# Six weight loads issued ahead of a barrier, and weight splitting and ranks reordered, in a sparse-attention and mixture-of-experts kernel

## What is computed

```python
h = _layernorm(x, axis=-1) * (1 + cb) + sb
x = x + gb * _L0_ffn_ref(h, router_w, router_b, w1, b1, w2, b2)

# in _L0_ffn_ref: 8 experts, 2 of them for each row
logits = xf @ router_w + router_b
topk_w, topk_i = jax.lax.top_k(jax.nn.softmax(logits, axis=-1), 2)
topk_w = topk_w / jnp.sum(topk_w, axis=-1, keepdims=True)
gates = zeros.at[rows, topk_i].set(topk_w)
h = jax.nn.relu(jnp.einsum('th,ehf->tef', xf, w1) + b1)     # 256 -> 1024
y = jnp.einsum('tef,efh->teh', h, w2) + b2                  # 1024 -> 256
out = jnp.einsum('te,teh->th', gates, y)
```

## Time and profile before

| | us |
|---|---|
| median of three runs | 1073.55 (1071.24 to 1073.58) |
| the profiled execution | 1073.43 |
| its span | 1071.6 |

### The profile page before, as it was taken

One profiled execution on the slowest core, in us unless ns is written; L12 is line 12 of the kernel. 1 busy time (PEld: TensorE's weight loads), 2 busy tenths in 40 slices (PEclk: granted clock), 3 DMA queues, 4 the chain that ended last, 5 costly groups with the idle time before them and its releaser, 6 DMA issues. The chain is left out here.

```text
span 1071.6 us, 26148 instructions
## 1 busy us (share of the span) xinstructions
PE 943.1 (88%) x7509; PEld 603.9 (56%) x7510; DVE 823.8 (77%) x2003; ACT 656.1 (61%) x1463; POOL 572.1 (53%) x582
## 2 busy tenths in 40 slices
PE   5998752699999999997688777999999999999995
PEld 3664442123333333332577336777788888888884
DVE  3677778789999999995667663777787777777773
ACT  3896776378988888886466583445444444444441
POOL 1347761737777777753766002444545445454533
PEclk9999995579999999998799697999999999999998
DMA  7126630521111111401587708988723323232322
GB/s 255 60 99 185 186 100 6 162 73 22 36 22 37 22 37 22 137 6 38 156 229 215 250 2 230 230 214 229 170 50 46 53 39 59 39 52 46 47 43 30
DMA packets 124954, 105.46 MB, mean 98 GB/s; under 512 B 17424, under 2 KB 118480, under 8 KB 124880
## 3 DMA queue, kind: packets, MB, share of 16 engines
q1 hardware_dynamic: 103024, 82.82, 25.9%
q0 software_dynamic: 20480, 20.67, 12.3%
q10 hardware_dynamic: 1376, 1.05, 0.3%
HBM read 50.13 MB, written 31.30 MB: 76 GB/s over the span
## 5 line engine op out<-in xcount | busy, mean ns | idle before, releaser
L1075 DVE TENSOR_REDUCE attend_mxh<-attend_p_a 128x1 f32<-128x512 f32 x416 | 257.1, 676 | 9.8 <-PE attend_p_a L1298 9.1
L2101 ACT ACTIVATE expert_hr<-expert_p,b1t 128x256 f32<-128x256 f32 (+1 forms) x376 | 134.1, 422 | 195.2 <-PE expert_p L2039 170.9
L1203 ACT ACTIVATE w<-attend_p_b 128x409 f32<-128x409 f32 x512 | 227.5, 515 | 37.4 <-PE attend_p_b L1312 35.4
L1994 POOL DMA_INDIRECT out_x<-expert_ys,expert_drop x72 | 125.1, 1738 | 190.5 <-DVE expert_ys L2136 136.6
L2061 PE MATMUL expert_p<-w,expert_hhi 128*128 x800 | 136.8, 273 | 0.7 <-DVE expert_ys L2136 0.3
L2039 PE MATMUL expert_p<-expert_xhi,w 128*128 128x256 f16 x800 | 136.4, 273 | 0.0
L1312 PE MATMUL attend_p_b<-attend_qb,w 64*128 64x409 f16 x512 | 130.8, 345 | 1.5 <-ACT w L1203 1.0
L1298 PE MATMUL attend_p_a<-w,attend_qa 64*128 64x512 f16 x384 | 123.5, 406 | 2.1 <-DVE attend_mxh L1075 1.3
L1984 POOL DMA_INDIRECT expert_xs<-h_d,expert_take x72 | 73.0, 1014 | 85.8 <-DVE expert_take L2140 64.8
L1338 PE MATMUL attend_p_o<-w,attend_vh 128*32 128x409 f32 x1024 | 116.4, 527 | 1.7 <-issue 0.7
L2061 PE MATMUL expert_p<-w,expert_hlo 128*128 x400 | 109.0, 273 | 0.0
(11 more groups left out here) (386 smaller groups left out, 1842.9 us busy)
## 6 DMA issues: line engine op xcount, KB each, us to landing
expert_wu<-w SPq DMA_DIRECT2D x88, 256.0 KB, 3.9
w<-in_L_ffn_w SPq DMA_DIRECT2D x30, 512.0 KB, 7.0
w<-in_L_attn_x SPq DMA_DIRECT2D x8, 512.0 KB, 10.9
q_d<-q SPq DMA_DIRECT2D x32, 128.0 KB, 1.7
k_d<-w SPq DMA_DIRECT2D x32, 128.0 KB
w<-k_d SPq DMA_DIRECT2D x32, 128.0 KB
attn_d<-zero SPq DMA_DIRECT2D x8, 512.0 KB, 5.8
route_ain<-attn_d SPq DMA_DIRECT2D x32, 128.0 KB, 3.6
```

Of the source, the lines that this page charges most:

```text
L1075: dve.tensor_reduce(mxh[q % 2][:, h, c, k:k + 1], p_a[chunk_use(q, a, h) % CB][:, :], AX, ALU.max).then_inc(a_done, 1)
L1203: act.activation(prob[:, 2 * (j % (TPB // 2)) + h, :], p_b[tile_use(p, j, h) % TB][:, 0:TOP], ACT.Exp, scale=SCALE / UNIT ** 2).then_inc(p ...
L1994: pool.indirect_dma_start(out=out, out_offset=bass.IndirectOffsetOnAxis(ap=drop[u][:, s:s + 1], axis=0), in_=ys[u][:, s, :], in_offset=Non ...
L2101: last = act.activation(hr[g % 2][:, f, rows], p_1[g][:, f, rows], ACT.Relu, bias=cst["b1t"][:, bass.ds(e[s] * FB + 2 * g + f, 1)], scale= ...
```

## The change

`w_here`, the semaphores on which the 12 weight loads land, and `raw_at` move from the slots block to `route_block` itself, as a set of their own that `places` hands out and clears. The first six loads are issued by SP in the routing block, behind its last save of h2 and ahead of its waits for the saves; the other six stay in the slots block. On ACT, Exp moves from behind piece 2 to behind high(1), and pieces up to high(7) and low(6) are done ahead of the tables; high(8) and low(7) stand between the tables where high(7) and low(6) stood. On PE, `LEFT_AT` becomes `(0, 0, 7, 7, 8, 9, 9)`: no piece ahead of the ranks and the far transpose, seven ahead of the spare product, none at group 0, one at group 1, one at group 2, none at group 3, three behind.

```diff
+        LOADS = [e * PIECES + c for e in range(E // 2, E) for c in range(PIECES if e < E - 2 else 2)]
+        AHEAD, SOON = 2, 6
+        _, _, kept_sem = places(nc, own, "weights")
+        w_here = [kept_sem(f"w_here{i}") for i in range(len(LOADS))]
+
+        def raw_at(n):
+
+            e, c = divmod(LOADS[n + AHEAD], PIECES)
+            if c < 2:
+                return cst["w1"][:, e, c, :, :].rearrange("p a f -> p (a f)").bitcast(F32)
+            return cst["w2"][:, e, (c - 2) * FB // 2:(c - 1) * FB // 2, :, :].rearrange("p b a n -> p (b a n)").bitcast(F32)
...
                 pipeline(sp, [load, None, None, None, save, None, None, save_h])
+                for n in range(SOON):
+                    sp.dma_start(raw_tile(raw_at(n), LOADS[n]), raw_of(io, LOADS[n])).then_inc(w_here[n], 16)
                 for c in range(4):
                     sp.wait_ge(h2_saved[c], 16 * NT // 4)
                     sp.wait_ge(x2_saved[c], 16 * NT // 4)
...
-            LEFT_AT = (1, 1, 6, 7, 7, 8, 8)
+            LEFT_AT = (0, 0, 7, 7, 8, 9, 9)
...
-                    for n in range(len(LOADS)):
+                    for n in range(SOON, len(LOADS)):
                         load(n)
...
-                    weights(0, 3)
+                    weights(0, 1)
+                    high(1)
                     act.wait_ge(dl_done, 1)
                     act.activation(ex[:, :], dl[:, :], ACT.Exp).then_inc(ex_done, 1)
-                    weights(3, 7)
+                    low(0)
+                    weights(2, 8)
                     act.wait_ge(slots_done, 1)
                     for g in range(GROUPS):
...
                         if g == 0:
-                            high(7)
+                            high(8)
                         if g == 1:
-                            low(6)
-                    for n in range(8, len(LOADS) + 1):
+                            low(7)
+                    for n in range(9, len(LOADS) + 1):
                         if n < len(LOADS):
                             high(n)
                         low(n - 1)
```

More of the change, by code:

```diff
@@ L1666, in route_block @@
             rank_ps, dl_done, ex_done = sem("rank_ps"), sem("dl_done"), sem("ex_done")
-            LOADS = [e * PIECES + c for e in range(E // 2, E) for c in range(PIECES if e < E - 2 else 2)]
             HALVES, WCOLS = 2, WCH // 2
-            LEFT_AT = (1, 1, 6, 7, 7, 8, 8)
-            AHEAD = 2
+            LEFT_AT = (0, 0, 7, 7, 8, 9, 9)
             wlast = [sb(f"wlast{i}", [P, WCH], F32) for i in range(AHEAD)]
+            raw_of_load = [raw_at(n) for n in range(len(LOADS) - AHEAD)] + [w[:, :] for w in wlast]
             p_w = [ps(f"p_w{i}", [P, 512], F32) for i in range(4)]
[L1674 to L1683, removed]
+            w_high, w_left, w_low = sem("w_high"), sem("w_left"), sem("w_low")
             def part_half(i, part, q):
@@ L1700, in load @@
                     def load(n):
-                        sp.dma_start(raw_tile(raw_at(n), LOADS[n]), raw_of(io, LOADS[n])).then_inc(w_here[n], 16)
-                    for n in range(len(LOADS)):
+                        sp.dma_start(raw_tile(raw_of_load[n], LOADS[n]), raw_of(io, LOADS[n])).then_inc(w_here[n], 16)
+                    for n in range(SOON, len(LOADS)):
                         load(n)
@@ L1714, in high @@
                         wait(act, w_left, HALVES * (n - AHEAD + 1))
-                        act.activation(weight_part(cst, LOADS[n], 0), raw_tile(raw_at(n), LOADS[n]), ACT.Copy, scale=WSCALE).then_inc(w_high, 1)
+                        act.activation(weight_part(cst, LOADS[n], 0), raw_tile(raw_of_load[n], LOADS[n]), ACT.Copy, scale=WSCALE).then_inc(w_high, 1)
                     def low(n):
@@ L1757, in left @@
                                 into = bank_half(HALVES * n + q, LOADS[n])
-                                raw = raw_at(n)[:, q * WCOLS:(q + 1) * WCOLS]
+                                raw = raw_of_load[n][:, q * WCOLS:(q + 1) * WCOLS]
                                 pe.matmul(into, minus[:, :], raw if LOADS[n] % PIECES < 2 else raw.rearrange("p (b n) -> p b n", n=D), start=True, stop=False)
```

## The result

The changed kernel takes 1078.77 us (median of 7, 1077.27 to 1081.19), the kernel before 1073.46 (median of 7 with the three from above, 1070.1 to 1075.47). The ratio is 1.0065, 95% interval 1.0052 to 1.0078: slower by 0.5 to 0.8%. The forecast was 1079.7.

A forecast was written before the change was run, and what follows sets the result against it. The prediction took the weight pieces on ACT and PE to set the slots block's end. +5.7 us at that end and +0.6 for the further clear made +6.3 on 1073.4: 1079.7 us, range 1073 to 1083.5.

The forecast's parts named there:

- What bounds the block: Slots block: the weight pieces on ACT and PE, not the routing, set the end, 4.1 us behind DVE.
- SP's six loads: Six loads issued ahead of SP's waits for the saves open the barrier later: +0.9 us, between 0.5 and 1.3.
- Ranks first, worth 0: Rank matmuls ahead of piece 0 put DVE's chain 3.45 us ahead, less 0.9; worth 0 on the path.
- A: Start of ACT's lane table 0: 621.7 instead of 618.6, +3.1 us, between 620.6 and 622.6.
- Behind A: Tables and tail: new wait at low(7), half clock in pieces 7 and 9, one piece fewer (-2.15); with A, +5.7 us.
- The further clear: The 12 semaphores' own set needs another clear with a barrier: +0.6 us, between 0.4 and 0.9.
- The table load: Ahead of Exp on ACT: load takes 1.28 us, without the skill page's 1.38 us drain; with it, forecast 1.4 us less.
- The gaps between bursts: PE between pieces 8 and 9: the skill's advice against idle gaps speaks against the change; clock down again, 1.75 us.
- Rival 1: Clock holds: pieces 7 and 9 on PE run at full clock, total 1075.1 us; chance 0.22.
- Rival 2: DVE's lead passes through: the block's end hangs on the routing chain, -4.1 us, total 1069.4; chance 0.09.
- Rival 3: SP hangs at one of the six issues, barrier opens 2.6 us later still, total 1082.3 us; chance 0.08.
- Rival 4: Nothing moves: waits at the block's ends swallow the change, total 1073.5 us; chance 0.05.

The follow-up runs named there:

- the version with two loads: Kernel before plus two early loads, semaphores from the slots block's set, ACT doing high(0), high(1), low(0), then Exp: ratio 0.9976 to before, run again 0.9975.
- one clear: Changed kernel with the 12 semaphores taken from the slots block's own set, so no further clear and barrier: ratio 1.0054 to the kernel before.

## Why the prediction was right, point by point

- **What bounds the block** held: the weight pieces end it. ACT's last copy ends 4.6 us behind DVE's drop table (648.90 against 644.34), and ACT began lane table 0 at least 1.1 us behind DVE's last slots in every run, so in none did DVE's lead decide when the tables begin.
- **SP's six loads**: forecast +0.9, measured +1.58. The mechanism was right, and the term too small. Six issues took 3.48 us, 0.58 each, where I took 0.46 from the loads in the slots block. The first two behind the saves take 0.46 each here too (0.92 in the version with two loads); it is the later ones that take longer, and why is open. The 1.3 that I gave as the upper bound was too low.
- **Ranks first, worth 0**: right. The matmuls ran at 603.29 and DVE's wait for them is gone, and lane table 0 did not come with it.
- **A**: forecast 22.94 + 2.2 behind DVE's start, measured 25.05. Its closeness is in part luck: in six more executions with seven pieces ahead it was 23.6 to 25.2, and in the five of them with ranks first 24.7 at most. The spread is the clock's first rise: from the first piece to A it was 18.26 us where the clock rose 5.1 us behind that piece (the changed kernel) and 16.80 where it rose 2.1 us behind (one clear). The parts of the term: the piece more cost 2.06 in its own run, and ranks first 0.3 behind DVE's start, with an early rise. Against them stands the stall that Exp caused ahead of piece 3 in the kernel before,

```profile
611.37 1.13 PE L1759 MATMUL slots_p_w<-w,minus 128*128 128x512 f32 x2 [1.03 <-ACT w L1715]
```

  of which there is none in the changed kernel, as forecast. So the move of Exp gave back about 1 us; it was not run alone.
- **Behind A**: table 3, piece 9 and the end were forecast 12.4, 16.2 and 25.3 behind, and came at 12.34, 16.56 and 26.07. The wait at low(7) was there, with piece 7 at half clock for 3.9 us (626.65 to 630.58) as forecast. How long the half clock lasted there was the mis-sized part: piece 9 starts 4.22 us behind table 3 instead of the forecast 3.8, and the pieces from it on lost 2.2 us, where I let them lose the 1.75 of piece 7, since the clock came back only at 643.8. The five executions with the wait at low(7) and no small matmuls end 25.8 to 26.1 behind A, though table 3 starts 12.3 behind it in three of them and 13.3 in two: the first and the second dip share the loss differently.
- **The further clear**: forecast 0.6, measured 0.87, inside its bounds of 0.4 and 0.9. The row that I took begins at the release of the barrier before and covers one clear; in the changed kernel the two clears begin 0.9 us apart (POOL's drains at L80, 649.1 and 650.0).
- **The sum** was +6.3; the block of the profiled execution grew by 7.9, the span by 7.4, the medians by 5.3. By the block, then, the terms were 1.6 us too small in all (0.7 SP, 0.8 behind A, 0.3 the clear, -0.1 A). That the total came within 1 us of the median all the same is luck in part: the profiled execution was 2.1 us above its median and had the latest first rise of the clock of all with ranks first, and no trace shows where a median execution is shorter. On another chip the same kernel was 9.2 us over before. In the first trace of the changed kernel the experts gave back 1.05 us: 429.4 us from their first copy to the span's end before, 428.3 after; their clock rose 4.6 us after their first matmul instead of 6.0.
- **The table load.** In the version with two loads it stands between a copy that ends at 602.03 and Exp, as in the earlier trace rows:

```profile
602.05 1.28 ACT L1739 ACT_TABLE_LOAD   x1
...
603.34 0.23 ACT L1739 ACTIVATE slots_ex<-slots_dl 128x32 f32<-128x32 f32 x1
```

  Exp starts 0.01 us behind the load. The drain of 1.38 us that the Trainium skill (ScalarE: Activation LUTs, What ACT_TABLE_LOAD costs) adds is on neither side of it; the measurement decides.
- **The gaps between bursts.** Filling them gave 4.3 us back. The advice of the Trainium skill (TensorE: Matmul & The Clock Gate, Why this matters for your kernels) to leave no long idle gaps between bursts of matmuls agrees with that.

Rival 1 (the clock holds) did not come by itself; made to hold, it gave the 21.79 that is near the 21.8 of its sum. Rival 2 (DVE's lead) is refuted. Rival 3, SP hanging at one issue, did not occur: 3.48 us for six. Rival 4, nothing moves, is out by the interval.

## What to carry to other kernels

Ask of every piece of work that is moved ahead who stands behind it in program order: here one more piece ahead of four tables and the wait between them that came with it cost 5 us, and a lead of 2 to 4 us on DVE was worth nothing, since another engine was late at that point already. Issues put in front of a barrier are free only as far as the wait behind them is long: two DMA issues fitted, six did not. And an early load is worth something only if an engine takes it at once. TensorE's idle gaps carry a price that shows only in the work behind them, so put the next piece there, or, as here, even products that nobody reads, and look at the granted clock of the stretch.

## What the runs showed of the hardware that I had not expected

Small matmuls whose result nobody reads made a stretch of the changed kernel faster: 24 of them (48 rows of about 0.27 us, which overlap) took 4.3 us off it, for the granted clock stayed at 1.00.

The rise of the clock came 2.1 to 5.6 us behind the start of the block's first piece in the thirteen profiled executions: 5.1 in the changed one, 4.1 in its second execution, 2.1 in the one with one clear (with ranks first, their products had begun 1.3 us ahead of the piece), and 5.4 in the kernel before. Each microsecond of it costs half a microsecond (18.26 against 16.80 us from the piece to A, for 3.0 us of delay), and this alone moves the block by up to 1.5 us between executions of like kernels.

And the time from issue to use of a load differs: two loads issued at 590.90 let ACT start at 595.65, 4.75 us behind, where the first of the kernel before took 3.9. The first two were issued right behind a save; whether that is the reason was not tested.
